# Expert rows in 64 full tiles and 8 mixed tiles of two 64-row halves, in place of 79 full tiles

## The reference, cut to what matters

```
scores = softmax(xt @ gate_w.T)            # 16 experts, in 4 groups
# the 2 best groups are kept, then the K = 4 best experts of a token; weights normed
out = 0
for e in range(16):
    a = silu(g) * u   where  g, u = split(xt @ expert_up_w[e].T)      # 512 -> 2 x 352
    out += cw[:, e:e+1] * (a @ expert_down_w[e].T)                     # 352 -> 512
out += swiglu(xt @ shared_up_w.T) @ shared_down_w.T
```

## Time and profile before

| | us |
|---|---|
| median of three runs (lowest, highest) | 1313.72 (1310.14, 1315.01) |
| span of the profiled execution, first to last instruction | 1306.4 |
| PE busy | 1264.5 (97%) |
| DVE busy | 872.4 (67%) |
| ACT busy | 375.1 (29%) |
| POOL busy | 340.0 (26%) |
| PE matmuls of the experts: G, U, D | 199.9, 199.9, 229.4 |
| granted PE clock, mean | 0.989 |

### The profile page before, as it was taken

One profiled execution on the slowest core, in us unless ns is written; L12 is line 12 of the kernel. 1 busy time (PEld: TensorE's weight loads), 2 busy tenths in 40 slices (PEclk: granted clock), 3 DMA queues, 4 the chain that ended last, 5 costly groups with the idle time before them and its releaser, 6 DMA issues.

```text
span 1306.4 us, 27873 instructions
## 1 busy us (share of the span) xinstructions
PE 1264.5 (97%) x8725; PEld 787.1 (60%) x8726; DVE 872.4 (67%) x2430; ACT 375.1 (29%) x822; POOL 340.0 (26%) x398
## 2 busy tenths in 40 slices
PE   8969999999999999999999999999999999999997
PEld 7857778777775555444444555555555555555553
DVE  4897688768768465262111777777777777777774
ACT  4745655645553333210000111111111111111111
POOL 1301234313242231225651112121212122121212
PEclk9989999999997999999999999999999999999999
DMA  5524944743643694585467456666665656564420
GB/s 163 95 47 99 157 94 101 166 105 85 138 109 114 169 199 116 124 274 199 182 211 246 85 130 138 134 137 137 137 139 133 135 132 136 127 139 72 75 49 9
DMA packets 208516, 171.09 MB, mean 131 GB/s; under 512 B 71472, under 2 KB 160560, under 8 KB 208432
## 3 DMA queue, kind: packets, MB, share of 16 engines
q1 hardware_dynamic: 135056, 114.16, 33.9%
q0 software_dynamic: 16496, 34.23, 13.4%
q10 hardware_dynamic: 56880, 21.54, 7.9%
HBM read 91.06 MB, written 82.73 MB: 133 GB/s over the span
## 4 chain that ended last, share of the span: by engine, by line
PE 55%; DVE 2%; issue 0%; DMA 0%; POOL 0%; ACT 0%; DVEq 0%; POOLq 0%
PE pD L2314 15%; PE pG L2289 14%; PE pU L2298 14%; PE pG L2246 3%; PE pU L2246 3%; PE pD L2265 3%; PE pU L2240 1%; PE pD L2260 0%; DVE ups L2187 0%; DMA out<-y,ix 0%; DVE w L1887 0%; DVE w L1888 0%; DVE route_keep L1886 0%; POOL out L2079 0%; DVE qf L1899 0%
## 5 line engine op out<-in xcount | busy, mean ns | idle before, releaser
L2187 DVE STREAM_TRANSPOSE ups<-a 32x96 f32<-32x96 f32 (+1 forms) x1248 | 326.1, 261 | 42.5
L2079 POOL DMA_INDIRECT out<-y,ix x79 | 123.0, 1557 | 479.1 <-ACT y L2140 319.4
L2314 PE MATMUL pD<-w,ups 128*128 (+1 forms) x474 | 216.6, 592 | 0.7 <-DVE ups L2187 0.7
L2289 PE MATMUL pG<-w,xsT 128*128 x632 | 199.9, 458 | 0.0
L2298 PE MATMUL pU<-w,xsT 128*128 x632 | 199.9, 459 | 0.0
L2289 PEld LDWEIGHTS pG<-w,xsT 128*128 128x128 f32 x632 | 119.5, 189 | 88.4 <-issue 37.4
L2298 PEld LDWEIGHTS pU<-w,xsT 128*128 128x128 f32 x632 | 120.1, 190 | 66.9
L976 PE MATMUL pProj<-front_region 128*128 128x256 f32 x624 | 154.8, 391 | 2.2 <-ACT front_region L711 1.6
L2314 PEld LDWEIGHTS pD<-w,ups 128*128 128x128 f32 (+1 forms) x474 | 90.0, 190 | 93.2 <-issue 76.8
L976 PEld LDWEIGHTS pProj<-front_region 128*128 128x128 f32 x624 | 113.3, 191 | 20.1 <-ACT front_region L711 2.1
L2140 ACT ACTIVATE y<-pD,wq 128x512 f32<-128x512 f32 x79 | 54.3, 687 | 247.0 <-PE pD L2314 234.1
(11 more groups left out here) (258 smaller groups left out, 1661.8 us busy)
## 6 DMA issues: line engine op xcount, KB each, us to landing
w<-in_up_T SPq DMA_DIRECT2D x16, 1408.0 KB
slot_rows<-zeros SPq DMA_DIRECT2D x79, 266.0 KB
xs<-slot_rows ACTq DMA_DIRECT2D x316, 64.0 KB
w<-in_down_T SPq DMA_DIRECT2D x16, 512.0 KB
front_region<-in_L_attn_hidden_states SPq DMA_DIRECT2D x16, 256.0 KB, 3.6
x2r<-in_L_attn_hidden_states SPq DMA_DIRECT2D x16, 256.0 KB, 4.5
partial_sums<-x2r SPq DMA_DIRECT2D x16, 256.0 KB, 2.9
x_normed<-x2n SPq DMA_DIRECT2D x16, 256.0 KB, 2.0
```

The lines of the kernel that those rows point to most:

```text
L2079: pool.indirect_dma_start(out=flat, out_offset=bass.IndirectOffsetOnAxis(ap=ix[1 - par][:, 0:1], axis=0), in_=y[1 - par][:, :], in_offset= ...
L2187: dve.transpose(aT[par][B * to:B * to + B, 0:n, rows], a[rows, 0:len(IC) * P].rearrange("p (c n) -> p c n", c=len(IC))[:, 0:n, B * to:B * ...
L2289: mm = pe.matmul(pG[0][:, 0:I], xsT[par][:, k, :], w[:, bass.ds(slot, 1), 2 * I * k:2 * I * k + I], start=(k == 0), stop=(k == DC - 1))
L2314: mm = pe.matmul((pYlast if end(q) else pYq)[:, :], aT[1 - par][0:m, c, :], down[0:m, :, UPW + D * c:UPW + D * (c + 1)], start=(c == 0), s ...
```

## The change

There are now 72 slots: NF = 64 full ones and NM = 8 mixed ones, every ninth (`q % 9 == 7`). Rows of an expert are counted in halves of 64. Pairs of halves go to full slots; an odd last half goes to one half of a mixed slot, of which the other half belongs to another expert. A mixed slot therefore needs the weights of two experts. It has a weight buffer of its own (`wm`, two experts' weights, in the SBUF region of the shared expert), loaded by ACT in 14 DMAs: three pieces behind the `y` copy of each of the slots 0 to 3 of nine, two behind that of slot 4. Each piece reads its expert's number from a list first.

```diff
+NF = K * T // P
+NM = E // 2
+NQ = NF + NM
+STEP = NQ // NM
+MIXED = STEP - 2
+PIECES = 3
...
-        with eng.Fori(1, (NQ - 3) // 2) as pair:
-            body(2 * pair, 0)
-            body(2 * pair + 1, 1)
...
+        for q in range(NQ + 1):
+            body(q, q % 2)
...
+            def load_mixed(m, part):
+
+                for piece in range(PIECES * part, min(PIECES * part + PIECES, 2 * (DC + len(IC)))):
+                    h, c = piece % 2, piece // 2
+                    up, down = weights_from(act, "mixed", 2 * m + h)
+                    if c < DC:
+                        act.dma_start(wm[:, h, 2 * I * c:2 * I * c + 2 * I], up[P * c:P * c + P, :]).then_inc(s_wm, 16)
+                    else:
+                        n, at = IC[c - DC], UPW + D * (c - DC)
+                        act.dma_start(wm[0:n, h, at:at + D], down[P * (c - DC):P * (c - DC) + n, :]).then_inc(s_wm, 16)
...
+                if PIECES * (q % STEP) < 2 * (DC + len(IC)) and q < NQ:
+                    load_mixed(q // STEP, q % STEP)
...
+            def project(out, rows, q, weights, at):
+
+                if is_mixed(q):
+                    for k in range(DC):
+                        for h in range(2):
+                            half = slice(HR * h, HR * h + HR)
+                            mm = pe.matmul(out[half, 0:I], rows[:, k, half], wm[:, h, 2 * I * k + at:2 * I * k + at + I],
+                                           start=(k == 0), stop=(k == DC - 1))
+                    return mm
...
+                for h in range(2 if is_mixed(q - 1) else 1):
+                    to = ixm[h] if is_mixed(q - 1) else ix[1 - par]
+                    least(pool, s_add, 16 * (adds_before(q - 1) + h))
+                    pool.indirect_dma_start(out=flat, out_offset=bass.IndirectOffsetOnAxis(ap=to[:, 0:1], axis=0),
...
+                        if gr == 2 and c < 5:
+                            list_dve(dve, c)
```

More of the change, by code:

```diff
@@ L1781, with is_mixed, before_mixed, adds_before @@
 NE = E + 2
-NQ = K * T // P + E - 1
-assert NQ % 2 == 1
-NS = 3
-def routing(nc, es, counts, scratch, lg, xall, pos, qslot, qexp, tiles_to, s_pos, s_read, s_routed, route, s_xall):
+HR = P // 2
+NF = K * T // P
[3 more added lines that the diff above has]
+MIXED = STEP - 2
+NS = 3
+PIECES = 3
+def is_mixed(q):
+    return q % STEP == MIXED
+def before_mixed(q):
+    return max(0, (q + STEP - 1 - MIXED) // STEP)
+def adds_before(q):
+    return q + before_mixed(q)
+def block_of(q):
+    return NF + q // STEP if is_mixed(q) else q - before_mixed(q)
+assert sorted(block_of(q) for q in range(NQ)) == list(range(NQ))
+assert all(q == i + (i + 1) // 8 for q in range(NQ) if not is_mixed(q) for i in [block_of(q)])
+def routing(nc, es, counts, scratch, lg, xall, pos, lists, s_pos, s_read, s_routed, route, s_xall):
     def sb(name, shape, dt=F32):
@@ L1807, in routing @@
     cnt, seg, inc = part(E, NT), part(E, NT), part(E, NT)
-    nti, idle = sb("nti", [P, E], I32), sb("silu_first", [P, E])
-    nt, one_e, tinc, posf = part(E), part(E), part(E), part(NT, E)
+    hti, fti, idle = sb("hti", [P, E], I32), sb("fti", [P, E], I32), sb("silu_first", [P, E])
+    hf, ff, of, cumf, cumo, one_e = (part(E) for _ in range(6))
+    full_rows, odd_at, apart, over, posf = part(E), part(E), part(E), part(1), part(NT, E)
     pj, ids = part(NT, K), part(NT)
     idi = sb("idi", [P, NT], I32)
-    qi, qc = sb("qi", [1, NQ]), both[0:1, 0:NQ * E].rearrange("p (q e) -> p q e", e=E)
-    qf, q3 = sb("qf", [1, NQ]), sb("q3", [1, NQ])
+    qi, qc = sb("qi", [1, NF]), both[0:1, 0:NF * E].rearrange("p (q e) -> p q e", e=E)
+    qf, qa, q3 = sb("qf", [1, NF]), sb("qa", [1, NF]), sb("q3", [1, NF])
+    cap, had, some, nth, twice, le, lm, lo_ = (sb(n, [1, E]) for n in (
+        "cap", "had", "some", "nth", "twice", "list_e", "list_m", "list_o"))
+    done_i = sb("done_i", [1, E], I32)
     pre, tot = counts[:, 0:NT * E], counts[:, NT * E:2 * NT * E]
@@ L1914, in experts @@
+    return route_act, route_pool, route_pe, route_dve, list_dve
+def experts(nc, es, wup_d, wdn_d, xs_d, acc_d, x2n_d, xT_d, lg, pos, lists, region, wsh, route, sh, out):
     N = GN
@@ L1936, in experts @@
     wq, ix = [sb(f"wq{i}", [P, 1]) for i in range(2)], [sb(f"ix{i}", [P, 1], I32) for i in range(2)]
+    ixm = [sb(f"ix_mixed{i}", [P, 1], I32) for i in range(2)]
     def bank(n):
@@ L2121, in body @@
                     load_rows(1, 1)
-                if not (isinstance(q, int) and q >= NQ - 2):
+                if q < NQ - 2:
                     load_rows(q + 2, par)
@@ L2334, in program @@
         pos = es.enter_context(nc.sbuf_tensor("pos", [P, NT, K], I32))
-        qslot = es.enter_context(nc.sbuf_tensor("qslot", [1, NQ], I32))
-        qexp = es.enter_context(nc.sbuf_tensor("qexp", [1, NQ], I32))
-        tiles_to = es.enter_context(nc.sbuf_tensor("tiles_to", [1, E], I32))
+        lists = {name: es.enter_context(nc.sbuf_tensor(f"list_{name}", [1, n], I32)) for name, n in (
+            ("slot", NF), ("load", NF), ("expert", NF), ("source", E), ("until", E), ("mixed", E))}
         xs_d = nc.dram_tensor("slot_rows", (NQ * P, RW), F32, kind="Internal").ap()
```

276 lines of the change are left out of this document (176 added, 100 removed).

## The result

| | before | after |
|---|---|---|
| median of runs, us | 1312.79 (1310.14 to 1315.01, four runs) | 1296.44 (1293.37 to 1297.32, four runs) |
| profiled execution: span, us | 1306.4 | 1294.8 |
| start of the first G | 718.44 | 719.6 |
| first G to last G | 568.7 | 549.9 |
| last G to the end of the span | 19.3 | 25.3 |

The changed kernel takes 0.9879 of the time before, 95% interval 0.9859 to 0.9899: 1.2% faster. The prediction was 1291 us with a range of 1266 to 1324.

The account below looks back on a forecast made before the run. PE's matmul stream was taken to bound the slot loop. With seven slots removed, span 1306.4 - 51.2 + 6.3 + 0.4 + 17.5 + 2.0 + 3.6 - 1.6 = 1283.4 us; with 7.3 outside, 1291 us, range 1266 to 1324.

Parts of the forecast that it names:

- the likeliest case: Whole kernel: the forecast itself holds, with a time of 1278 to 1306 us; chance 0.42.
- the 15 us of that estimate: Eight mixed slots: halves overlapping only in part, at 79%, would cost 15 us more; partial overlap had chance 0.08.
- 7 meetings x 2.5 = +17.5: Loop slots where SP's expert load meets pieces: rows come late and PE stalls, 2.5 us each (0 to 6).
- The first pieces meet the storing of acc: +2: Slot 0: the first pieces' transfers compete with the storing of `acc`, adding 2 us.
- +6.3: Eight mixed slots: 32 changes between whole and half array at 0.20 us each; bounds nothing to 13 us.
- Alone, the pieces cost nothing: Slots with pieces but no expert load: rows arrive at 914 or 915, before 917.5, so no cost.
- +3.6 + 0.4: End of the kernel: one more addition in the final chain, 3.6 us, and two more array changes, 0.4 us.
- 7.3 us as lying outside the span: Whole kernel: median of runs above the profiled span before, kept and added to the predicted span.
- D to D above 7.4 us in slots without pieces: Slots 5 to 8 of nine: a sign of being wrong, since 7.31 us was expected there.
- The rival of pieces holding up ACT: Slots with pieces: ACT or DVE held up, up to 1.4 us in each of 40, time 1345; chance 0.24.
- The reserve of 0.6 us: Slots with pieces: what DVE's 1.7 us reserve leaves after `a` comes 1.1 us late, so ACT's issues cost nothing.
- The chain of additions: Slots where load and pieces meet: additions to `out` falling behind for two slots would raise a meeting to 6 us.

Follow-up runs that it names:

- tiny_expert_loads: Changed kernel with SP's 13 expert loads inside the loop cut to 64 bytes on 16 partitions each, mixed pieces whole: 1273.5 us, one run.
- whole_mixed: Changed kernel with mixed slots computed by whole matmuls of 128 columns in place of halves (wrong products): 1297.6 us, one run.
- ring4: Changed kernel with index and weight columns and `y` four buffers deep in place of two: 1297.0 us, 0.989 of the kernel before.
- tiny_pieces: Changed kernel with the 14 pieces of each mixed slot after the first still issued but carrying 64 bytes a partition: 1275.9 us, one run.
- two_per_slot: Changed kernel with two pieces a slot over seven slots, behind `y`, in place of three over five: 1356.0 us, 1.034 of the kernel before.

## Why the prediction was right, and where its sizes were off

It was right on the sign and on the likeliest case, and these steps of its working held. A mixed slot costs what a full one does but for the changes of shape: 5.4 us measured, 6.3 + 0.4 predicted. The 16 instructions of a G in pairs, 0.296 us a pair, settle the question of the Trainium skill's packing figure as well (TensorE: Matmul & The Clock Gate, Measured speedup vs the span model: three column tiles at 2.38 times): two column halves reach 2.0 here, so the 15 us of that estimate don't arise. The stall stands where SP's load meets the pieces, is ended by `xsT`, and the rows come 14.9 us after the first piece in the first meeting (14.6 predicted), where PE stood for 1.55 us (1.7 predicted). `g` starts 5.7 us or more behind `y` in most slots with pieces, where it was 3.6, so the 2 us of the prediction hold. The front gained its 1.6 us: from DVE's copy of the counts (L1868 before, L1902 now) to the first G it takes 141.2 us, where it was 142.8, and PE's wait of 1.6 us for the sum is gone.

The terms that were mis-sized, against the profiled execution's span (1283.4 predicted, 1294.8 measured, 11.4 apart), were these:

- "7 meetings x 2.5 = +17.5". Measured 26.2: six meetings at a mean of 4.4, +8.7 us. The number was one too high. The price was too low for two reasons. The lateness of the rows alone came to 19.4 of the 26.2 us, 3.2 each and not 2.5, with PE idle for up to 3.1 us. And I left out that such idle time can lower PE's clock, at 1.7 us each in four of the six. This is the one mechanism that is missing from the prediction. Its upper bound of 6 us for a meeting was passed by one, with 6.5.
- "The first pieces meet the storing of acc: +2". Measured 0.5.
- "+6.3": 5.4.
- "Alone, the pieces cost nothing", and nothing for ACT's issues: with the expert loads made small, the two together cost 4.6 us (tiny_expert_loads). In the changed kernel only about 1 us stands outside the meetings, half of it in the line on `acc`, so the term adds next to nothing to the sum below.
- The tail: +3.6 + 0.4 predicted, +6.0 measured. The three additions are 3.5 and 3.6 us apart, as said, but the end lay 8.5 us behind the last of them, where it was 6.2:

```profile
1279.30 1.56 POOL L2186 DMA_INDIRECT out<-y,ix_mixed  x1 [6.54 <-ACT y L2255]
1282.76 1.55 POOL L2186 DMA_INDIRECT out<-y,ix_mixed  x1 [1.90 <-DMA out<-y,ix_mixed]
1286.34 1.56 POOL L2186 DMA_INDIRECT out<-y,ix  x1 [2.02 <-DMA out<-y,ix_mixed]
```

- The first block, which the change doesn't touch, ended 2.8 us later in this execution (the copy of the counts starts at 578.46, before at 575.65). The start of the first G varies that much among the changed kernel and its twelve variants, from 717.0 to 720.4.

So 8.7 - 1.5 - 0.9 + 2.0 + 2.8 = 11.1 of the 11.4 us. Against it stood another error: I took 7.3 us as lying outside the span, from the median less the profiled span. The profiled execution of after has a time of its own, 1296.56, and only 1.8 us lie outside. With as much outside, the profiled execution of before took some 1308.2 us, so most of the 7.3 was that it was a short one among the runs. That 1291 lies within 6 us of the measured 1296.4 is thus partly luck: with 1.8 us the same sum gives 1285, 11 us below.

One of the signs of being wrong was set against the prediction's own sum. D to D above 7.4 us in slots without pieces did come (7.55, 7.51 and 7.57 around a mixed slot), but by the changes of shape that the sum had priced at 0.20 us each; whole_mixed brings the periods back to 7.31.

The rival of pieces holding up ACT was refuted as a steady cost, though ACT is as loaded as it said: DVE waits for `g` in 47 slots, and a row load's issue has a median of 0.453 us, where it was 0.327:

```profile
L2212 ACTq DMA_DIRECT2D xs<-slot_rows x288: 309/453/1484, 707.0 to 1256.1; - x144
```

The reserve of 0.6 us that I worked out was enough in most slots. The chain of additions, which I named as the upper end of a meeting's price, is refuted by ring4 for the changed kernel.

What stays open: why the clock fell at 956 us and not at 886 us, after the same idle time (over the changed kernel and its variants the shortest idle time before a G with a fall right behind it was 1.72 us, in tiny_pieces, and the longest without one 2.58 us, in two_per_slot); what makes up the longer end behind the last addition; and which part of a meeting's lateness is bytes in the queue ahead of the rows and which the sharing with SP's load (both go when either is made small).

## What to carry to other kernels

When an engine has next to no idle time, price an added wait with the lower clock that it can bring, and look for it in the granted clock behind each wait: a stall of 2.3 us cost 4. Put bulk transfers on a queue behind the small load that someone waits for, at the point where the small one has just left, and check the deadline of the last bulk piece before spreading them. Here, moving the pieces from behind `y` to behind `g` took 14 to 16 us off, while spreading them behind `y` added about 10 over six slots and 60 over seven. A deeper buffer on a serial chain may only move its wait to the end of the program.

## What the runs showed of the hardware

- Two column halves of the matrix array, 128 x 64 each, stream 352 fp32 columns at once at full speed: the two of a pair start 7 ns apart, and a pair takes 0.296 us, as one whole instruction does. A change between whole and half array costs 0.17 us (0.68 us for four), near the 0.20 of the row halves.
- With the halves one behind the other in the program, matmuls of U's first half are recorded as starting ahead of three of G's second half. The Trainium skill (TensorE: Matmul & The Clock Gate, The mechanism) has matmuls strictly in the order of the program; the recorded starts across two halves of the array differ.
- A clock that had been at its full level for over 500 us (from 407 to 957 us of the span) fell to 0.50 after PE had been idle for 2.29 us (at 955.60), and 1.7 us of work were lost before it was back. After the same idle time at 886.28 it did not fall.
- A row-load issue on ACT has a median of 0.453 us in the changed kernel, 0.327 before, and took up to 1.85 us beside SP's expert load in tiny_pieces.
